# Plain row-major weights in HBM in place of pre-tiled ones, and ternary weights stored in halves, in a layer-norm, scan and BitLinear kernel on 8 cores

## The reference

```python
x = x + attn_ref(layernorm(x), A, W_b, b_b, W_c, b_c, D, W_t, b_t, W_o, b_o)
x = x + ffn_ref(layernorm(x), fast_b, w_fc, w_proj, u, v, gate)

# attn: delta = sigmoid(x W_t) * 0.99 + 0.01;  h = scan(exp(A delta), x W_b);  y = (h W_c + x D) W_o
def bitlinear(x, w):                      # w_fc [4096, 1024], w_proj [1024, 4096], float32
    scale = clip(mean(abs(w), axis=1), 1e-5)
    tern = clip(round(w / scale), -1, 1)
    return x @ (tern * scale).T           # in value
def ffn_ref(x, ...):
    h = bitlinear(x, w_fc) + gate * (x @ v.T @ fast_b.T @ u.T)
    return bitlinear(maximum(h, 0) ** 2, w_proj)
```

## Time and profile before

| | us |
|---|---|
| median of 3 runs (2051.82 to 2104.03) | 2052.01 |
| profiled execution | 2053.46 |
| its span on the slowest core (4); others 2038.2 to 2050.1 | 2051.9 |
| TensorE busy, share of the span | 1382.9 (67%) |
| VectorE busy | 896.1 (44%) |
| ScalarE busy | 332.5 (16%) |
| bytes moved by DMA, mean rate | 221.43 MB, 108 GB/s |

### The profile page before, as it was taken

How to read it: one execution, slowest core, us unless ns; L and a number is a source line. 1 busy time by engine, 2 the same in 40 slices (tenths; PEclk the granted TensorE clock), 3 DMA queues, 4 the chain that set the end, 5 groups by cost and what they waited for, 6 DMA issues and landing times.

```text
span 2051.9 us, 14848 instructions; the slowest of 8 cores (2038.2 to 2051.9 us)
## 1 busy us (share of the span) xinstructions
PE 1382.9 (67%) x5768; PEld 619.6 (30%) x5768; DVE 896.1 (44%) x933; ACT 332.5 (16%) x392; POOL 26.9 (1%) x42
## 2 busy tenths in 40 slices
PE   0544465324288859884987489758966896698598
PEld 0211155301033314331433134223422342243243
DVE  1677778745623271237124621552164316413410
ACT  1111122101131013101300230022003200210220
POOL 0000000000000000000000000000000000000000
PEclk9766677656599979996998699879977997899799
DMA  5232244341021513141324123412431151235123
GB/s 128 102 119 106 118 169 172 118 160 40 1 103 64 203 41 124 65 181 41 123 82 164 62 103 107 166 52 86 160 128 59 65 185 62 72 113 185 38 106 143
DMA packets 34324, 221.43 MB, mean 108 GB/s; under 512 B 4512, under 2 KB 4512, under 8 KB 13760
## 3 DMA queue, kind: packets, MB, share of 16 engines
q1 hardware_dynamic: 21296, 167.79, 22.8%
q0 software_dynamic: 12960, 52.69, 7.3%
HBM read 189.28 MB, written 33.55 MB: 109 GB/s over the span
## 4 chain that ended last, share of the span: by engine, by line
PE 57%; DVE 27%; issue 6%; DMA 5%; ACT 4%; DVEq 0%; POOL 0%; POOLq 0%; ACTq 0%; SPq 0%
PE pb L961 21%; PE pb L906 21%; PE pb L764 5%; PE pb L354 3%; PE pb L436 2%; DVE tls L617 2%; DVE tls L875 2%; DVE xnb L627 2%; DVE xnb L885 2%; DVE cb L380 2%; DVE sqbuf L547 2%; DVE cb L381 2%; DMA woT_b<-woT 2%; PE pb L555 1%; DMA wsl<-wprojT 1%
## 5 line engine op out<-in xcount | busy, mean ns | idle before, releaser
L906 PE MATMUL pb<-xnb,wcmb_st 128*128 128x512 bf16 x2048 | 470.9, 394 | 137.1 <-DVE but L653 80.6
L961 PE MATMUL pb<-r2b,wproj_st 128*128 128x512 bf16 x2048 | 443.6, 379 | 0.7 <-DMA wproj_st<-wproj_sc 0.7
L906 PEld LDWEIGHTS pb<-xnb,wcmb_st 128*128 128x128 bf16 x2048 | 205.3, 101 | 402.7 <-issue 180.3
L961 PEld LDWEIGHTS pb<-r2b,wproj_st 128*128 128x128 bf16 x2048 | 200.2, 98 | 242.7 <-issue 2.0
L936 DVE TENSOR_TENSOR r2b<-r2b 128x4096 bf16<-128x4096 bf16 x32 | 73.3, 2292 | 388.1 <-ACT r2b L927 388.1
L979 DVE TENSOR_TENSOR xn<-xn,pb 128x512 f32<-128x512 f32 x64 | 44.0, 687 | 365.7 <-PE pb L961 365.7
L927 ACT ACTIVATE r2b<-pb 128x512 bf16<-128x512 f32 x256 | 152.1, 597 | 289.9 <-PE pb L906 289.8
L764 PE MATMUL pb<-yb,woT_b 128*128 128x512 bf16 x512 | 127.4, 412 | 17.7 <-DVE yb L743 12.9
L852 ACT ACT_TABLE_LOAD x8 | 10.3, 1283 | 699.8 <-DVE statB L846 699.8
L555 PE MATMUL pb<-xb,ones_b 128*128 128x512 bf16 x64 | 28.2, 620 | 124.9 <-DVE xb L548 124.9
L304 PE MATMUL pb<-GTb,v_b 16*128 16x512 bf16 x64 | 22.1, 450 | 113.6 <-DVE wr L311 113.5
(11 more groups left out here) (108 smaller groups left out, 1138.0 us busy)
## 6 DMA issues: line engine op xcount, KB each, us to landing
wcmb_st<-wcmb_sc SPq DMA_DIRECT2D x64, 1024.0 KB, 4.8
wproj_st<-wproj_sc SPq DMA_DIRECT2D x64, 1024.0 KB, 5.0
x_s<-xT POOLq DMA_DIRECT2D x8, 2048.0 KB, 8.5
yT<-xn POOLq DMA_DIRECT2D x8, 2048.0 KB, 8.9
wsl<-wfcT SPq DMA_DIRECT2D x4, 2048.0 KB, 8.4
wslB<-wfcT SPq DMA_DIRECT2D x4, 2048.0 KB, 8.9
wcmb_sc<-wr POOLq DMA_DIRECT2D x8, 1024.0 KB, 4.1
wsl<-wprojT SPq DMA_DIRECT2D x4, 2048.0 KB, 8.7
```

What stands on the lines that cost most here:

```text
L906: i2 = te.matmul(pb[b][:], wcmb_st[:, hs % 2, dc, (hc % 4) * 128:(hc % 4 + 1) * 128], xnb[:, p, dc], start=(dc == 0), stop=(dc == DCH - 1))
L961: i2 = te.matmul(pb[b][:], wproj_st[:, oc % 2, kc, :], r2b[:, kc], start=(kc == 0), stop=(kc == hch - 1))
```

## The change

wfcT and wprojT become plain transposes [1024, 4096] and [4096, 1024], and the rearrangement moves from the host into the access pattern of the loads: a slice of w_fc is now 1024 runs of 2 KB, a slice of w_proj 4096 runs of 512 B. The stores of the ternary slices become two DMAs each, with a second pair of semaphores, `s_sa0` and `s_sa1`, for the first halves; for w_fc the first half is issued after the fourth of the eight additions, for w_proj both are issued one after the other once the slice is done. Whoever waited for a store now waits for both halves.

```diff
-    wfcT = nc.dram_tensor("wfcT", [nhs, 128, DCH, TT], F32, kind="ExternalInput").ap()
-    wprojT = nc.dram_tensor("wprojT", [DCH, 128, hch, 128], F32, kind="ExternalInput").ap()
+    wfcT = nc.dram_tensor("wfcT", [D, h], F32, kind="ExternalInput").ap()
+    wprojT = nc.dram_tensor("wprojT", [h, D], F32, kind="ExternalInput").ap()
...
+    def sca_sem(j):
+        return "s_sa%d" % (j % 2)
...
                 wadd_hist[(hs, dc)] = ctr["s_V"]
             blk.vector(_wadd)
+            if dc == 3 or dc == DCH - 1:
+                half = 0 if dc == 3 else 1
+                sem = sca_sem(hs) if half == 0 else scw_sem(hs)
+                w = ctr["s_V"]
+
+                def _wr(g, hs=hs, half=half, sem=sem, w=w):
+                    wait(g, "gpsimd", "s_V", w)
+                    assert inc(g.dma_start(
+                        out=wcmb_sc[hs, :, 4 * half:4 * half + 4],
+                        in_=wr8[:, hs % 2, 4 * half:4 * half + 4]),
+                        sem, 16) == scw_count(hs)
+                blk.gpsimd(_wr)
         slice_c_done[hs] = ctr["s_V"]
-
-        def _wr(g, hs=hs):
-            wait(g, "gpsimd", "s_V", slice_c_done[hs])
-            assert inc(g.dma_start(out=wcmb_sc[hs], in_=wr8[:, hs % 2]),
-                       scw_sem(hs), 16) == scw_count(hs)
-        blk.gpsimd(_wr)
...
-            inc(sy.dma_start(out=wv[:], in_=wfcT[hs]), wldq(hs), 16)
+            inc(sy.dma_start(
+                out=wv[:],
+                in_=wfcT[:, hs * TT:(hs + 1) * TT].rearrange("(c p) h -> p c h", p=128),
+            ), wldq(hs), 16)
...
             if hs >= 2:
+                wait(ve, "vector", sca_sem(hs - 2), scw_count(hs - 2))
                 wait(ve, "vector", scw_sem(hs - 2), scw_count(hs - 2))
...
-            inc(sy.dma_start(out=wv2[:], in_=wprojT[os_]), wldq(j), 16)
+            inc(sy.dma_start(
+                out=wv2[:],
+                in_=wprojT[:, os_ * 128:(os_ + 1) * 128].rearrange("(c p) o -> p c o", p=128),
+            ), wldq(j), 16)
...
             wait(g, "gpsimd", "s_V", slice2_c_done[os_])
-            assert inc(g.dma_start(
-                out=wproj_sc[os_],
-                in_=wr8[:, j % 2].rearrange("p c (a b) -> p (c a) b", b=128)[:, 0:hch, :]),
-                scw_sem(j), 16) == scw_count(j)
+            wrv = wr8[:, j % 2].rearrange("p c (a b) -> p (c a) b", b=128)[:, 0:hch, :]
+            hh = hch // 2
+            assert inc(g.dma_start(out=wproj_sc[os_, :, 0:hh], in_=wrv[:, 0:hh]),
+                       sca_sem(j), 16) == scw_count(j)
+            assert inc(g.dma_start(out=wproj_sc[os_, :, hh:hch], in_=wrv[:, hh:hch]),
+                       scw_sem(j), 16) == scw_count(j)
```

More of the change, by code:

```diff
@@ L161, in build_nc @@
                  "s_wc0", "s_wc1", "s_wp0", "s_wp1", "s_sc0", "s_sc1",
-                 "s_wl0", "s_wl1", "s_sml", "s_T", "s_V", "s_S"]:
+                 "s_sa0", "s_sa1", "s_wl0", "s_wl1", "s_sml", "s_T", "s_V", "s_S"]:
         sems[name] = nc.alloc_semaphore(name)
@@ L459, in _cmp2 @@
             if j >= 2:
+                wait(ve, "vector", sca_sem(j - 2), scw_count(j - 2))
                 wait(ve, "vector", scw_sem(j - 2), scw_count(j - 2))
@@ L543, in _sq @@
                 wait(ve, "vector", "s_sc1", sc1_total)
+                wait(ve, "vector", "s_sa0", sc0_total)
+                wait(ve, "vector", "s_sa1", sc1_total)
             if j >= 1:
@@ L1004, in _wsA0 @@
         wait(sy, "sync", "s_sc1", sc1_total)
+        wait(sy, "sync", "s_sa0", sc0_total)
+        wait(sy, "sync", "s_sa1", sc1_total)
         for hs in range(2):
@@ L1047, in make_in_maps @@
                  fast_b, w_fc, w_proj, u, v, gate, spc=SEQ_PER_CORE):
-    nhs_, hch_ = w_fc.shape[0] // TT, w_fc.shape[0] // 128
     shared = dict(
[L1050 to L1053, removed]
+        wfcT=np.ascontiguousarray(w_fc.T),
+        wprojT=np.ascontiguousarray(w_proj.T),
         woT=np.ascontiguousarray(W_o.T),
```

## The result

| | us |
|---|---|
| changed kernel, median of 38 runs | 2056.46 |
| kernel before, median of 38 runs, by turns on the same chips | 2053.74 |
| ratio, with its 95% interval | 1.0013 (1.0007 to 1.0019) |
| forecast: ratio, and range | 1.005 (2062 on 2052), 2046 to 2082 |

The time lies in the range, and it rose as forecast, but by 2.7 us (1.4 to 3.9) and not by 10: the size is off by a factor of nearly four. Eleven of the 38 executions before and seven after took 2 to 10% more, with the cores of one die or of both at a lower granted clock; the ratio leaves them out.

What follows compares the result with a forecast made beforehand. No engine is full; serial work binds, with three wprojT loads whole on the proj part's chain. Loads +13.2, start -3 and split stores +0.5 sum to +10.7, say +10 on 2052: 2062 us, range 2046 to 2082.

Steps and rivals of the forecast that it cites:

- the size of the wprojT loads: Proj part: each 512 B-run load grows by 4.4 us (1.3 to 7.3); three count, +13.2 us (3.9 to 21.9).
- the upper bound: wprojT loads: 0.043 us per 512 B packet, 10.9 us an engine, 5.5 us more per load.
- the lower bound: wprojT loads: 0.0265 us per packet as for 64 B packets, 6.8 us an engine, 1.3 us more per load.
- The store's 1.0 us: Proj part: even loads give way to the previous slice's store running beside them, 1.0 us more each (0 to 1.8).
- Three loads on the path, whole: Proj part: of eight wprojT loads three lie whole on the chain, 8.99, 8.91 and 8.45 us long.
- The wfcT loads cost nothing: Fc part: 2 KB runs add 0.5 us an engine, covered by 8.8 us, so costed at nothing; uncovered 3 us.
- a sign of being wrong: Fc part: the prediction is wrong, beyond its rivals, if this part's 211.5 us changes by over 2 us.
- The start, -3: Start: woT gets more turns beside 2 KB packets and lands earlier, -3 us (from a 1 us loss to 8 gained).
- The split stores, +0.5: End of proj part: one more POOL store issue of 0.53 us delays the first x_s load, +0.5 us.
- A: wprojT loads: rival that 512 B runs cost the load nothing, 2049 or 2046 us; chance 0.18.
- B: Start: rival that it gives most of its 8 us as woT passes the weights, 2058 us; chance 0.15.
- C: wprojT loads: rival that SP's queue or memory can't keep up, slower by over 2%, 2085 us; chance 0.15.

Runs made afterwards that it cites:

- e6: Changed kernel with wprojT laid out so that a load comes in 16384 runs of 128 B: ratio 1.0243, +50 us.
- e1: Kernel before with wprojT alone in plain rows, runs of 512 B; wfcT stays tiled, stores stay whole: ratio 1.0023, 4.7 us.
- e4: Changed kernel with one more wait: GpSimd stores w_proj slice j only after the load of slice j+2 has landed: ratio 1.0013.
- e3: Changed kernel with both weights tiled again, leaving only the split stores of the change: ratio 1.0000.
- e9: Changed kernel with a third buffer for the weight slices, loads from slice 9 on issued one slice earlier: ratio 0.9936.
- e10: e9 with wprojT tiled again, wfcT in rows and stores split: ratio 0.9931.
- e5: Changed kernel with wprojT laid out so that a load comes in 8192 runs of 256 B: ratio 1.008, +16 us.
- e7: Kernel before with woT on its own semaphore, issued after slice 1's load landed, awaited only before tile 0's output projection: ratio 0.9938, 12.7 us gained.
- e8: Changed kernel with woT on its own semaphore, issued after slice 1's load landed: ratio 0.9906, 19.3 us gained.

## Why the prediction was right or wrong

- **The step that failed: the size of the wprojT loads.** The prediction put 4.4 us on a load, from the middle between 1.3 and 5.5 us for the packets and 1.0 for the store. Measured over eight cores and three slices the load grew from 8.76 to 10.05 us, 1.3 us, and three of them make 3.9 us and not 13.2. The middle was the mistake, since the upper bound was wrong.
- **Why the upper bound was wrong.** It came from a line through x_s's 4 KB packets and the 16 KB packets of SP, two different queues, and from their packet durations. The mean of 0.1875 us holds the start of that load: the first 49 of its 512 packets took 0.36 us each, while the median packet took 0.165. A line through 0.165 and the 16 KB packet's 0.71 has no fixed part at all, so the price per packet that the prediction read from it was the start of the load.
- **The right reading** takes the packets of SP's queue alone: the changed kernel moved 3883 of 512 B in 6.7 us, 6.7 x 16 / 3883 = 0.0276 us each; the kernel before moved 124 of 16 KB in 5.5 us (the row below), 0.71 us each. An engine needs 7.1 us for a load in place of 5.7, close to the 6.8 of the lower bound from the 64 B packets, 0.0265 us each. That it fitted so well is partly luck: in e6 SP's 128 B packets took 0.013 us each in their records (47.6% x 32 x 16 / 18381, window 280 to 312), half as long as those 64 B packets of GpSimd's queue, so packet durations don't carry over from queue to queue.

```profile
q1 hardware_dynamic: 124, 2.03, 96.4%
```

- **The three loads did not grow alike:** it was 0.8 us for slices 10 and 14 and 2.25 for slice 12, whose late engines were told above. How much of the growth is due to the 4 KB from run to run, and not to the 512 B, no run shows.
- **The two rules that the prediction cited.** The Trainium skill's rule on small descriptors (DMA: Bandwidth & Descriptors, Why small descriptors are slow) gave under 1.1 us a load. The trace agrees roughly with it: 0.8 us for slices 10 and 14, 1.1 for slices 8 and 9, 1.4 by the engine time above. The Trainium skill's rule of full rate from 512 B on (same page, Specifications) the trace bears out in part only: by it the short runs would cost nothing, and e1 measures 4.7 us.

- **The store's 1.0 us in it** was wrong as well: with the store moved away the loads take as long (e4), and split stores alone leave them as they are (e3). The prediction let the load of slice 10 last until 294, with the whole store inside; it was over at 290.35, before the store's packets mattered.
- **Three loads on the path, whole: right.** e9 and e10 show it from one side, e5 and e6 from the other. But not all of 3.9 us arrived. The proj part grew by 3.1, since TensorE's sums of slices 10, 12 and 14 became shorter, from 9.40, 9.72 and 9.91 us to 9.77, 9.22 and 9.23 in the mean, together 0.8. The windows of two of them, before and then changed (stretch, length, then busy time of PE, PEld, DVE, ACT and POOL, and behind them the granted clock):

```profile
330.70:340.80 10.10, 10.01 (x64) 9.85 (x64) 5.29 (x3) 1.21 (x1) 0.53 (x1) 0.73 0.78 294
364.40:374.70 10.30, 10.23 (x64) 10.06 (x64) 5.39 (x3) 1.48 (x2) 0.53 (x1) 0.71 0.82 277
```

```profile
331.70:340.90 9.20, 9.12 (x64) 8.93 (x64) 3.61 (x2) 0.66 (x1) 1.05 (x2) 0.80 1.08 311
365.40:374.80 9.40, 9.31 (x64) 9.15 (x64) 4.60 (x3) 0.18 (x1) 1.05 (x2) 0.78 0.98 269
```

  The same 64 matmuls met a mean clock of 0.80 and 0.78 in place of 0.73 and 0.71, a mix of the levels of 1.2 and 2.4 GHz. What raised it no run shows, and the prediction had no term for it.
- **The wfcT loads cost nothing: right** within what the fc part shows, 212.5 against 211.6, where e1 and e7 with tiled wfcT have 212.0 and 212.3. On the slowest cores alone the part is 2.3 us longer (213.8 against 211.5), past the 2 us that the prediction named as a sign of being wrong, but these are two different cores.
- **The start, -3: right in sign and mechanism**, 2.0 us measured over ten profiles. On core 5 woT was in at 36.2 us, ahead of the last packet of the second wfcT load at 37.6. L261 began at 36.17 on the slowest core (forecast: about 36, from 39.30), though part of that is which core was slowest.
- **The split stores, +0.5: wrong in sign, small.** The tail got shorter by 1.5 us in the profile, and by about 0.9 over all profiles with split stores (18.6 to 19.5, but 20.2 in e10) against those without (19.8 to 20.4). In the changed kernel's timeline

```profile
405.70 0.91 POOL L527 DMA_DIRECT2D x_s<-xT  x1
410.74 0.91 SPq L1029 DMA_DIRECT2D wcmb_st<-wcmb_sc  x2
422.08 4.42 DVE L568 TENSOR_TENSOR sqbuf<-x_s 128x4096 bf16<-128x4096 f32 x1 [17.96 <-DMA x_s<-xT]
```

  the x load goes 0.5 us later after its store, as forecast, but lands after 16.3 us and not 18.1. SP's weight loads begin 5.0 us behind it, in place of 4.1. The prediction named this help to x_s and set it to nothing. That it is the cause was not tested, and e3's time, 1.0000, shows neither.
- **The rivals.** A (512 B costs nothing) falls to e1, though it was nearer to the truth than the forecast's 4.4. B, an 8 us start, falls: 2.0. C, a queue that can't keep up, falls at 512 B; e6 shows it at 128 B, where the issue of the load of slice 11 took 4.24 us while that of slice 10 was under way.

## What to carry to other kernels

Before a layout is tiled on the host for longer DMA runs, ask whether the load is on the path at all: here 32 times shorter runs cost 1.3 us a load on three loads, and nothing that shows once a third buffer covered them: the proj part then took 125.3 us with either layout, in place of 138.3 and 141.4. When a price lies between two bounds of different kind, take the row from the same queue, and reckon it from the bytes moved in a window and not from packet durations, before taking the middle. And look for small constants that share the DMA engines with large packets: once woT was out of the way, half a KB queued behind 64 B packets decided the start. Where several loads count on one semaphore, read the packets and not the landing of one of them.

## What the runs showed of the hardware

- A 2 MB load from SP took 8.8 us in 16 KB runs, 10.05 in 512 B, 14.4 in 256 B and 22.3 in 128 B, means over eight cores and three slices, some of them beside other traffic. With the engines nearly free (slices 8 and 9) it was 8.3, 9.5 and 12.4 us for the first three. No run had short runs without the pitch of eight runs, so the two aren't told apart.
- Engines served two queues about one packet each in turn (134 beside 145 in 8 us), and a queue was the slower, the larger the packets of the other: the last of 1024 packets of 64 B ended at 21.5 us beside 16 KB packets (e7) and at 11.2 beside 2 KB packets (e8), means of eight cores. The Trainium skill (DMA: Bandwidth & Descriptors, Queues, rings and completion order) states the turns by packet; the trace agrees.
- A load was as late as its last engine: in slice 12 of the changed kernel 14 of 16 engines were through 9.2 us after the issue and the last at 11.1, with two instruction packets in the load; without such packets the 14th and the last were 0.05 us apart (slice 10).
- The proj part was 136.2 to 136.5 us on three cores and 139.3 to 139.7 on the other five of one execution of the kernel before, and 125.3 to 125.4 on all eight in e10, where no load is on its path. What parts the two groups no run shows.
